# One sequence's top slots carried over unmerged, the last picks split five and three, and one row sum moved between the two averages

## The reference, cut to what matters

```python
# block 1, x is layer-normed before it
r = sigmoid(x @ Wr.T); k = x @ Wk.T; v = x @ Wv.T
scaled = k * v / clip(scale, 1e-10)            # scale = exp(pos * log_decay)
out = r * (cumsum(scaled, axis=1) * scale)
mean, var = mean and variance of out over (T, D), one pair per sequence
normed = (out - mean) * rsqrt(var + 1e-5) * gn_weight + gn_bias
x = x + normed @ Wo.T
# block 2, on layernorm(x), 2048 tokens flat
logits = xf @ w_router.T                       # E = 64 experts
top_vals, top_idx = top_k(logits, 4); w_tok = softmax(top_vals)
# each expert keeps its first C = 64 tokens in token order
order = argsort(e_flat); tok_ec, w_ec = the first 64 (token, weight) of each expert
y = (silu(x_ec @ w_gate) * (x_ec @ w_up)) @ w_down      # I = 384, per expert
out = x + scatter_add(y * w_ec) + shared expert
```

## Time and profile before

| what | us |
|---|---|
| three runs | 717.33, 714.2, 716.8; median 716.8 |
| the profiled execution, its own time | 719.23 |
| its span in the profile | 717.4 |
| TensorE matmuls busy | 669.6 (93% of the span) |
| VectorE busy | 333.5 (46%) |
| GpSimd busy | 222.2 (31%) |
| ScalarE busy | 161.0 (22%) |
| mean granted TensorE clock | 0.986 of full |

### The profile page before, as it was taken

How to read it: one execution, slowest core, us unless ns; L and a number is a source line. 1 busy time by engine, 2 the same in 40 slices (tenths; PEclk the granted TensorE clock), 3 DMA queues, 4 the chain that set the end, 5 groups by cost and what they waited for, 6 DMA issues and landing times. The chain is left out here.

```text
span 717.4 us, 9017 instructions
## 1 busy us (share of the span) xinstructions
PE 669.6 (93%) x3229; PEld 404.4 (56%) x3229; DVE 333.5 (46%) x809; ACT 161.0 (22%) x259; POOL 222.2 (31%) x209
## 2 busy tenths in 40 slices
PE   3999999999699998999999999999999999999980
PEld 2587878888588754554554554554554554444330
DVE  5887567759967782233232332332323223232220
ACT  4833115623111321112111111111111111121110
POOL 4637546446546313002111022112202022111111
PEclk9999999999899999999999999999999999999996
DMA  8201015713636898499999999999999999999973
GB/s 322 66 1 59 1 30 198 259 57 133 249 143 267 294 337 304 159 366 357 406 404 387 370 388 392 400 398 365 395 393 404 353 402 391 393 399 372 388 256 41
DMA packets 52347, 202.67 MB, mean 282 GB/s; under 512 B 7331, under 2 KB 7459, under 8 KB 51920
## 3 DMA queue, kind: packets, MB, share of 16 engines
q1 hardware_dynamic: 36512, 169.23, 59.6%
q0 software_dynamic: 8928, 21.33, 12.5%
q10 hardware_dynamic: 6864, 11.54, 4.3%
HBM read 178.66 MB, written 23.59 MB: 282 GB/s over the span
## 5 line engine op out<-in xcount | busy, mean ns | idle before, releaser
L618 POOL DMA_INDIRECT out_dram<-ym,midx x32 | 51.3, 1602 | 303.0 <-DVE ym L1245 123.7
L1583 PE MATMUL bank<-w_sb,xT 128*64 128x384 f32 x768 | 129.1, 489 | 0.8 <-ACT xT L841 0.8
L1369 PE MATMUL bank<-x_hi,w_parts 128*128 128x512 f32 x368 | 118.1, 404 | 4.1 <-DVE x_lo L954 3.2
L1604 PE MATMUL bank<-w_sb,guT 128*64 128x512 f32 x384 | 88.0, 593 | 2.9 <-DVE ym L1245 1.6
L1583 PEld LDWEIGHTS bank<-w_sb,xT 128*64 128x64 f32 x768 | 53.0, 137 | 63.8 <-issue 60.1
L1369 PEld LDWEIGHTS bank<-x_hi,w_parts 128*128 128x128 f32 x368 | 71.5, 195 | 20.8 <-DVE x_lo L954 4.0
L1369 PE MATMUL bank<-x_lo,w_parts 128*128 128x512 f32 x184 | 72.0, 400 | 0.0
L1185 DVE TENSOR_TENSOR gu<-sg,bank 128x384 f32<-128x384 f32 x32 | 17.7, 554 | 109.0 <-issue 101.9
L1504 PE MATMUL bank<-sh_sb,xS 128*128 128x384 f32 x192 | 63.9, 486 | 0.0
L1604 PEld LDWEIGHTS bank<-w_sb,guT 128*64 128x64 f32 x384 | 27.7, 137 | 51.5 <-issue 51.5
L1504 PEld LDWEIGHTS bank<-sh_sb,xS 128*128 128x128 f32 x192 | 35.7, 191 | 22.3
(11 more groups left out here) (184 smaller groups left out, 959.8 us busy)
## 6 DMA issues: line engine op xcount, KB each, us to landing
w_sb<-in_L_ffn_w_down SPq DMA_DIRECT2D x64, 768.0 KB
w_sb<-in_L_ffn_w_gate SPq DMA_DIRECT2D x48, 768.0 KB
w_sb<-in_L_ffn_w_up SPq DMA_DIRECT2D x48, 768.0 KB
extra<-in_L_ffn_w_gate SPq DMA_DIRECT2D x16, 768.0 KB
extra<-in_L_ffn_w_up SPq DMA_DIRECT2D x16, 768.0 KB
ring<-in_L_attn_x SPq DMA_DIRECT2D x14, 256.0 KB, 3.6
xt_dram<-xwT ACTq DMA_DIRECT2D x12, 256.0 KB, 3.2
xS<-xt_dram SPq DMA_DIRECT2D x12, 256.0 KB, 13.0
```

Source lines behind the costliest of these rows:

```text
L618: pool.indirect_dma_start(out=out[:, :], out_offset=bass.IndirectOffsetOnAxis(ap=midx[j % 3][u][:, :], axis=0), in_=ym[u][:, :], in_offset ...
L1369: ins = pe.matmul(ps[u][:, :], w, xp, start=(n == 0), stop=(n == len(parts) - 1))
L1583: ins = pe.matmul(ps[e * C:(e + 1) * C, 0:I], xT[:, c, e * C:(e + 1) * C], gate_up(2 * j + u, e, k)[:, c, :], start=(c == 0), stop=(c == K ...
L1604: ins = pe.matmul(pair_bank(j, u)[e * C:(e + 1) * C, :], guT[0][:, c, e * C:(e + 1) * C], down(2 * j + u, e)[:, c, :], start=(c == 0), sto ...
```

## The change

It does four things in three places. The first sequence's `best_rounds` writes its lists into the extra 64 columns of the keys on all 128 partitions, and the move, the copy and the merge are dropped; each half then carries its own 64 into the second sequence's search. The last picks take five tiles and three where they took four and four; `picked` gives the cut. And row_w is no longer summed from Wo in fp32 behind step 0 but from wo_hi and wo_lo in float32r, eight matmuls between `average(0, 0)` and `average(0, 1)`, into `ps_t[0]`; ScalarE copies it behind the last `out_high` of the first sequence. A new tile `ones_r` of 32 bytes a partition stands ahead of all later tiles.

```diff
+        ones_r = tile("ones_r", [P, 1], F32R)
-        cand = tile("cand", [E, 2 * C], at=xin_at + 1024)
+        def picked(b, h):
+            cut = (TILES // 2, TILES // 2 + 1)[b]
+            return slice(h * cut, TILES if h else cut)
 # GpSimd
+            pool.wait_ge(const_ready, 2)
+            pool.tensor_copy(ones_r[:, :], ones[:, :])
 # ScalarE, output_weights
-                act.activation(row_w[:, :], ps_v[1][:, :], ACT.Copy).then_inc(rows_copied, 1)
-                act.wait_ge(rows_ready, 2)
 # ScalarE, behind the first sequence's steps
             out_high(STEPS - 1)
+            act.wait_ge(rows_ready, 2)
+            act.activation(row_w[:, :], ps_t[0][:, :], ACT.Copy).then_inc(rows_copied, 1)
             turned_x(TILES)
 # VectorE, best_rounds
-                    found = best[:, 8 * k:8 * k + 8]
+                    found = best[:, 8 * k:8 * k + 8] if b else key[:, HALF + 8 * k:HALF + 8 * k + 8]
 # VectorE, between the steps
                 elif s == STEPS + 5:
-                    halves_together()
-                    merge_rounds(range(4))
-                elif s == STEPS + 6:
-                    merge_rounds(range(4, 8))
-                    seq.then(dve.memset(key[E:P, HALF:], -1.0))
                     seq.then(dve.tensor_scalar(ramp[:, :], ramp[:, :], -float(T), None, ALU.add))
 # TensorE
-                for ps, vector in ((ps_v[1], gnw_sb), (ps_k[1], gnb_sb)):
-                    (four fp32 matmuls for each)
+                (four fp32 matmuls for gnb_sb into ps_k[1])
+            def output_row_w():
+                pe.wait_ge(xlo_ready, TILES)
+                pe.wait_ge(const_ready, 3)
+                for c in range(KC):
+                    for part in (wo_hi, wo_lo):
+                        ins = pe.matmul(ps_t[0][:, :], ones_r[:, :].to_broadcast([P, P]), part[:, c, :],
+                                        start=(c == 0 and part is wo_hi), stop=(c == KC - 1 and part is wo_lo))
+                ins.then_inc(rows_ready, 1)
                 average(b, 0)
+                if b == 0:
+                    output_row_w()
                 average(b, 1)
 # TensorE, turn_xw(0)
-                    pe.wait_ge(xlo_ready, TILES - 1)
+                    pe.wait_ge(rows_copied, 2)
 # TensorE, behind step STEPS + 5
-                if s == STEPS + 5:
-                    move_best(0)
```

More of the change, by code:

```diff
@@ L1021, in pick @@
             def pick(b, h):
-                tiles = slice(h * TILES // 2, (h + 1) * TILES // 2)
+                tiles = picked(b, h)
                 dve.wait_ge(logit_copied, b * TILES + tiles.stop)
@@ L1033, in pick @@
                 dve.tensor_tensor(wgt[:, tiles, :], logits[:, tiles, 0:E],
-                                  top8[:, tiles, 0:1].to_broadcast([P, TILES // 2, E]), ALU.subtract).then_inc(diff_ready, 1)
+                                  top8[:, tiles, 0:1].to_broadcast([P, tiles.stop - tiles.start, E]), ALU.subtract).then_inc(diff_ready, 1)
                 dve.wait_ge(diff_ready, 2 * b + h + 1)
@@ L1055, in best_rounds @@
                 for k in rounds:
-                    found = best[:, 8 * k:8 * k + 8]
+                    found = best[:, 8 * k:8 * k + 8] if b else key[:, HALF + 8 * k:HALF + 8 * k + 8]
+                    if b and k == C // 8 - 1:
+                        dve.max(found, keys).then_inc(best_ready, 1)
+                        dve.wait_ge(best_ready, 1)
+                        break
+                    seq.then(dve.max(found, keys))
                     if k < C // 8 - 1:
-                        seq.then(dve.max(found, keys))
                         seq.then(dve.match_replace(keys, found, keys, -1.0))
-                    else:
-                        dve.max(found, keys).then_inc(best_ready, 1)
-                        dve.wait_ge(best_ready, b + 1)
             def weight_sums(b):
@@ L1067, in weight_sums @@
                 dve.reciprocal(wsum[:, :, :], wsum[:, :, :]).then_inc(sums_ready, 1)
[L1069 to L1081, removed]
             dve.wait_ge(ident_steps, 1)
@@ L1217, in _ @@
             dve.wait_ge(xw_stored[0], 16 * SEQS * TILES // 4)
-            dve.wait_ge(best_moved, 2)
+            dve.wait_ge(best_moved, 1)
             seq.then(dve.tensor_tensor(slots[:, :], best[0:E, :], ps_u[0][0:E, C - 1::-1], ALU.max))
@@ L1318, in output_rows @@
                 pe.wait_ge(raw_in[3], 16)
-                for ps, vector in ((ps_v[1], gnw_sb), (ps_k[1], gnb_sb)):
[L1320 to L1323, removed]
+                for c in range(KC):
+                    ins = pe.matmul(ps_k[1][:, :], gnb_sb[:, c:c + 1].to_broadcast([P, P]), raw[3][:, c, :],
+                                    start=(c == 0), stop=(c == KC - 1))
+                ins.then_inc(rows_ready, 1)
+            def output_row_w():
+                pe.wait_ge(xlo_ready, TILES)
+                pe.wait_ge(const_ready, 3)
+                for c in range(KC):
+                    for part in (wo_hi, wo_lo):
+                        ins = pe.matmul(ps_t[0][:, :], ones_r[:, :].to_broadcast([P, P]), part[:, c, :],
+                                        start=(c == 0 and part is wo_hi), stop=(c == KC - 1 and part is wo_lo))
+                ins.then_inc(rows_ready, 1)
             def first_of_second(i, half):
@@ L1357, in step @@
                     need(pe, free, s - 1)
-                    if s == 1 and i:
-                        pe.wait_ge(rows_copied, i)
+                    if s == 1 and i == 2:
+                        pe.wait_ge(rows_copied, 1)
                     parts = []
@@ L1424, in turn_masks, with move_best @@
                 pe.wait_ge(mask_ready, 2 * b + h + 1)
-                for i in range(TILES // 2):
-                    ins = pe.matmul(ps_t[0][h * E:(h + 1) * E, i * P:(i + 1) * P], mask[:, h * (TILES // 2) + i, :],
+                for n in range(picked(b, h).start, picked(b, h).stop):
+                    half, i = divmod(n, TILES // 2)
+                    ins = pe.matmul(ps_t[0][half * E:(half + 1) * E, i * P:(i + 1) * P], mask[:, n, :],
                                     ident_half[:, :], start=True, stop=True)
                 ins.then_inc(mask_turned, 1)
-            def move_best(b):
-                pe.wait_ge(best_ready, b + 1)
-                pe.matmul((ps_t[1], ps_u[0])[b][0:E, 0:C], ident[:, E:P], best[:, :], start=True, stop=True).then_inc(best_moved, 1)
+            def move_best():
+                pe.wait_ge(best_ready, 1)
+                pe.matmul(ps_u[0][0:E, 0:C], ident[:, E:P], best[:, :], start=True, stop=True).then_inc(best_moved, 1)
             pe.wait_ge(ident_steps, 2)
@@ L1544, in _ @@
             late_product(2, 0)
-            move_best(1)
+            move_best()
             turn_shared(1, ps_xt)
```

## The result

The changed kernel takes 709.98 us, the median of five runs (709.63 to 710.09), against 714.86 for the kernel before in the same comparison (five runs, 713.75 to 717.33): ratio 0.992, interval 0.9898 to 0.9942. (All ratios here are the estimates on record, with their 95% intervals; they are not the quotients of the two medians.) The profiled execution took 709.98, with a span of 708.2 where before it was 719.23 and 717.4. Median against median the change is worth 4.9 us, profiled execution against profiled execution 9.25. The experiments are about the gap between these two numbers.

What follows compares the result with a forecast made beforehand. TensorE was taken as the bound nearly everywhere. The terms -8.9 - 1.0 + 0.8 - 0.45 = -9.55 took the profiled execution from 719.23 to 709.7 and, against the median 716.8, gave 707.3 us, range 703.5 to 711.5.

Steps and rivals of the forecast that it cites:

- transfer to the median: Whole kernel: the profiled execution was 2.4 above the median of 716.8, so 709.7 profiled became 707.3 for the runs.
- Part 1: Between steps 13 and 14: without move and merge TensorE saves 6.95 of wait and 1.9 of half clock, -8.9 us.
- What is late next: Steps 14 and 15 to the average: VectorE back in front by step 15; a 2 us slip would cost 1.7.
- The cover at the average: At the average after step 15: aggregate ready at 209.3, TensorE arriving at 209.6, so 0.3 us to spare.
- Part 2: Step 0: row_w's eight records removed, 3.4 us off TensorE, of which 1.0 arrives (ends 0.5 and 3.4).
- The 0.4 taken for contention: VectorE's two wo_lo products near the start: some 0.4 us saved with GpSimd's work shifted against them.
- Part 3: Between the first sequence's averages: eight row_w matmuls take 1.9 us, partly hidden; cost 0.8 (ends 0 and 2.7).
- Part 4: Last pick before the experts: one tile less shortens TensorE's wait for the last mask, -0.45 us (0.2 to 0.67).
- A: Steps 14 and 15 or the average: VectorE or the clock still costs TensorE 2 to 4 us; 710.3, chance 0.10.
- B: Expert stage: transfers hold the end, 7 or more of the 9.5 us given back; about 715, chance 0.06.
- C: Weight stream: shifted slots slow it; 2.4% eats the gain, 4% gives 722.9; chance 0.04.
- D: Step 14: the wait only moves to another wait for VectorE; no chance of its own, counted in A.

Runs made afterwards that it cites:

- same_again: The kernel before, unchanged, profiled once more: 716.11 us, ratio 1.0004; its profiled execution took 714.34.
- late_weights: The kernel before with the 768 KB piece of down weights issued later, behind the wait for rscaled: 711.92 us, ratio 0.9938.
- extra_search_after: The changed kernel with three more searches of 512 keys on VectorE in step 11, results overwritten: 709.79 us, ratio 0.9926.
- part1_alone: The kernel before with only the first sequence's lists carried over, no move and no merge: 710.01 us, ratio 0.9909.
- without_part1: The changed kernel with move, copy and merge put back, split picks and moved row sum kept: 714.81 us, ratio 0.9984.
- row_w_in_two: The changed kernel with the row_w matmuls cut in two, four between the averages and four behind the second: 709.85 us, ratio 0.9923.
- changed_again: The changed kernel, unchanged, measured again in another group: 709.83 us, ratio 0.991.
- extra_search_before: The kernel before with three more searches of 512 keys on VectorE in step 11, results overwritten: 718.98 us, ratio 1.0058.

## Why the prediction was right, and where it was wrong

Forecast 707.3, range 703.5 to 711.5; measured 709.98, faster by 0.8%. The direction, the place and the mechanism hold. The size against the median, 9.5, was twice the 4.9 that came. The median of the kernel before moves from group to group (714.86, 716.82, 716.47, 714.77), and where the changed kernel was measured again it gained 6.6 (716.47 to 709.83).

**The failed step is the transfer to the median.** The sum said that the profiled execution goes from 719.23 to 709.7; the profiled execution of after took 709.98. That they agree so well is in part luck. Parts 2, 3 and 4 were to give 0.65 together and gave nothing at the last mask's turn (8.83 in all, where the sum had 9.55), and 0.45 came between the first expert product and the last scatter, where nothing was forecast and where executions differ by more than that (432.1 to 433.1, below). Then the prediction took off the 2.4 by which the old execution was above its median. That surplus was not a constant of profiling. Nearly all of it belonged to the very wait that the change removes, as the pair of executions 4.89 apart shows: the 6.4 of the earlier trace rows is one draw of a wait that is 2.2 in another execution of the same kernel and, with a faster store, 0.85. With the wait gone the surplus goes too, and an execution of after takes about 709.8 whatever the wait of before was (709.23 to 710.15 in 11 runs). The spread of the runs of before (714.2 to 717.33 for the three that were given) had shown that something in it was elastic, and the prediction named the 3 us only as noise. Its range was also summed short at the upper end: from 0.8 to part 3's upper end of 2.7 is 1.9, not 1.2, which makes 712.2. The measured time lies inside either.

**Part 1**, -8.9: from the turn at 112 (+0.09) to `project(8)` (-8.74) the profile gives 8.83. The term is right for this execution, half clock and all. For the medians it measured 6.8 and 6.3 (710.01 against 716.82, 710.17 against 716.47). The share of the half clock differs from draw to draw: from step 14's first matmul to `project(8)` it is 18.26 in before and 18.07 in same_again, against 16.45 in late_weights, where the clock stayed up. Step 14 starts 0.23 behind step 13 and the clock is 1.00, as said.

**What is late next:** nothing. The cover at the average (how long the aggregate is ready before TensorE needs it) was to be 0.3 and is 0.49. It does not shrink when VectorE is delayed (0.49 again in extra_search_after, 209.38 to 209.87), because VectorE waits for TensorE's delivery of step 15 and both set off from there. Taking a slip of VectorE as paid at the average was a misreading of the earlier trace rows: VectorE's true slack stands ahead of step 14 (2.24) and step 15 (3.88), and a delay of 5.3 us used up the first and 2.4 of the second with no loss.

**Part 2**, -1.0: mis-sized, it measured 0.66 at the first average in two executions whose first row matmul started alike (28.83 and 28.86). TensorE was handed 3.4 us, and VectorE did not follow:

```profile
41.35 1.41 DVE L945 TENSOR_SCALAR xn<-ring,mv,rstd 128x512 f32<-128x512 f32 x1 [0.73 <-POOL rstd L496]
42.67 1.50 DVE L968 TENSOR_SCALAR inv<-inv 128x512 f32<-128x512 f32 x1
44.09 1.40 DVE L1114 SCALAR_TENSOR_TENSOR wo_lo<-wo_raw,gnw_sb,wo_hi 128x512 fp32r<-128x512 f32 x2
```

The wait for x_hi, 0.56 in the earlier trace rows, is gone, and it is nearly the whole of the gain. The 0.4 taken for contention came to 0.13: wo_lo fell from 3.47 to 1.40, but the xn and inv ahead of it rose from 0.55 and 0.42 to 1.41 and 1.50. GpSimd's two products, at 42.52 to 45.60 before and 41.21 to 43.89 after, ran beside other operations of VectorE. TensorE's waits are 1.22, 0.79 and 0.77 where 0.5, 1.6 and 1.0 were forecast. Where the row matmuls start at 27.7 to 27.9 the gain is smaller still: the first average is at 100.58 in part1_alone (row sums behind step 0) and at 100.38 in without_part1 (row_w moved), 0.2 apart. In row_w_in_two, where they start at 28.01, it is at 100.66, with no gain at all. The kernel before started them at 27.87 in same_again, so the 28.83 of the earlier trace rows is a late start, and the 0.66 is worth less for other executions.

**Part 3**, +0.8: from the average (-0.66) to the turn (+0.09) it is +0.75. The second average is 2.07 behind the first, forecast 1.9, and 0.95 idle before the turn, forecast 1.1. ScalarE's copy was ready at 103.34, ahead of the row's product at 104.07. No row had shown the 0.1 taken for a switch; the eight matmuls took 1.93 from their first start to the second average (100.61 to 102.54).

**Part 4**, -0.45: not confirmed. The medians of two kernels are 0.64 apart, and the last mask's wait went from 1.20 to 0.87 where 0.7 to 0.8 was forecast. But from `project(8)` to the last mask's turn it is 38.19 before and 38.10 after, 0.09 less: the stage ahead of the wait lost the rest. In changed_again it is 37.98.

**The rivals.** *A* gave 710.3, the nearest number, for a reason that isn't there: no wait took the place of the old one. *B*: the distance from the first expert product to the last scatter was 432.88 and is 432.43, and the queue's wait for TensorE reads 227.0 us in 27. Nothing was given back. *C*: in 340 to 360 the stream moved 391 GB/s against 405, but that stretch now holds other experts, and the whole stage took no longer. The same distance is 432.11 to 433.13 in the eight profiled executions without the new tile and 432.32 to 433.09 in five with it (435.62 in extra_search_after, whose first product ran at half clock). So the tiles moved by 32 bytes cost nothing that shows. The rule of the Trainium skill (DMA: Bandwidth & Descriptors, How a descriptor splits into AXI transactions) is worded for the side that is read; for the weights that is DRAM, which did not move. Stores read from tiles that did move, and no run here tests the rule on them. *D* fell with the missing wait.

## What to carry to other kernels

A wait read from one profile is one draw. Before it goes into a sum, ask what starts the chain that it ends, and whether that start (here a store beside a weight load) has the spread that the runs show. If it does, and the change removes the wait, the time after is to be worked out from the profiled execution and left there, not shifted by that execution's distance to the median: the gain in the runs is smaller than in the profile by that distance. A second profile of the kernel before, 4.9 us faster than the first, would have shown it. An edit elsewhere may then buy most of the same gain: here one DMA issue behind one wait gave 0.62%.

## What the runs showed of the hardware

The landing of one store of 256 KB varied with the same program around it. ScalarE waited 6.97 and 4.98 for it in two executions of the kernel before, 5.26 and 7.29 in two of part 1 alone, 5.07 and 6.27 in two of the changed kernel. In the eleven profiled executions with the 768 KB load issued 0.45 us before the store the wait was 4.98 to 7.29, in the three without it 2.15, 4.08 and 4.49. The two sets do not overlap, so the load is part of it; what makes the rest vary stays open.

TensorE's clock does not follow the length of an idle stretch alone. After 6.38 idle it fell, and after 2.16 in same_again (eight matmuls 0.44 apart from 190.05, granted 0.91 in the window), but after 2.41 in without_part1 it did not. The 72 matmuls of steps 14 and 15 took 18.26 and 17.78 behind two idle stretches of 6.38 (before, extra_search_before), 18.07 behind 2.16, and 16.45 behind 2.41. The window of without_part1:

```profile
180.00:200.00 20.00, 17.59 (x79) 14.23 (x78) 16.90 (x37) 3.54 (x6) 10.41 (x10) 1.00 0.60 225
```

It also fell in one execution of the changed kernel with the three searches added. The profiled one of extra_search_after took 715.14 while its six others took at most 710.36. Its first gather came late, TensorE idled 2.49 and then 0.77, and the 32 matmuls behind took 7.86 us where they take 5.38 in the changed kernel's profile:

```profile
267.11 1.10 PE L1530 MATMUL bank<-ident,xg 128*128 128x128 f32 x4 [2.49 <-DMA xg<-xw_dram,pair_idx]
268.97 7.86 PE L1582 MATMUL bank<-w_sb,xT 128*64 128x384 f32 x32 [0.77 <-ACT xT L848]
...
260.00:280.00 20.00, 16.01 (x62) 7.69 (x61) 3.65 (x11) 2.18 (x4) 5.08 (x6) 0.83 0.66 223
```

So an elastic wait is left, the first gather. In the changed kernel's own profile it ended the last 0.78 us of TensorE's idle; in changed_again the same 0.78 was ended by ScalarE's `guT`; here it was 2.49. One of this kernel's seven runs paid for it, and none of the changed kernel's own 11 did (709.23 to 710.15). Whether the added searches had a part in it is open. The 714.37 of row_w_in_two may be the same; that run has no profile.
